# Second normalisation of a graph network: rows stored raw, factors kept, residuals normalised on load

## The chip, the core and the metric

The kernel runs on one core of a Trainium2 chip. The time is device time of one launch in microseconds. The core has a matmul engine (PE), a vector engine (DVE), a scalar engine (ACT), a general engine (POOL) that also builds the descriptors of indirect transfers, and SP, whose queue issues most plain transfers. Every engine works through its own instructions in order and meets the others through semaphores.

## The reference

There are N = 100,000 nodes with D = 128 features and E = 50,000 edges. Four residual blocks follow one another, each closed by a plain layer norm over the features:

```python
x = _layernorm(x + gcn2(x, edges))                 # block 0: two graph convolutions
x = _layernorm(x + gated(x, edges, edge_attr))     # block 1
x = _layernorm(x + attention(x, edges, edge_attr)) # block 2
x = _layernorm(x + gcn6(x, edges))                 # block 3: six convolutions, then @ Wf + bf

# gated: msg = sigmoid(z @ Wf.T + bf) * softplus(z @ Ws.T + bs); agg = sum of msg by dst
#        h = relu(LN(batchnorm(agg) + x) * gamma + beta);  returns h + x
# attention (3 heads): xp = x @ W; alpha = leaky_relu(a_src[row] + a_dst[col] + a_edge)
#        weights = softmax of alpha over the edges into a node (its own loop among them)
#        y = (sum of weights * xp[row] + bias) @ lin_W + lin_b;  returns LN(x + y) * g + b
```

Block 1 ends in two norms one after the other (its own, then the block's), and so does block 2. "First norm" and "second norm" below mean these two.

## The kernel before

Rows come in two kinds. The a rows (`rows_a`, 4 of 128 a block, 99 blocks `NBA`) are nodes with incoming edges, laid out with the sorted edges; the b rows (`rows_b`, 8 of 128 a block, 98 blocks `NB`) are all nodes, computed as if they had no edges. Both lie in one table, the b rows from row NA on. A block is 512 or 1024 rows.

The kernel is a chain of passes with a barrier after each. Every pass gives each engine a list of stages `(function, lag, blocks)` for `pipeline`: in turn t, stage f works on block t - lag, in the order of the list. So a stage's place is its lag (which turn) and its place in the list (where in the turn). Tiles have two, three or four buffers, and a semaphore wait with `b.after(k)` keeps k buffers apart. The passes and where they lie in the profiled span:

- first pass (0 to 666 us): sorts edges, makes weights (`weight_steps`, one product for each DVE turn), degree factors.
- graph passes 1 and 2 (to 2120.8): block 0.
- gated edge pass (to 2942.0): messages of block 1.
- gated node pass (`cn_`, to 4068.5): both norms of block 1 for a and b rows together, then transposes and the attention scores of each row. POOL has `batch_norm` and `gain`; DVE `stats_1`, `factors_1`, `shift`, `rectify`, `stats_2`, `factors_2`, `scores`; ACT `normalise_1`, `normalise_2` (both through `scale`, L1797, one activation for each 128 rows), the roots and `evacuate`; PE `turn` and `score`. `normalise_2` writes the tile o, which is stored as x2 and transposed.
- attention-gather pass (`ga_`, to 4856.6): b rows of block 2 (`AttentionNode` with `self_w`), while POOL gathers the scores of each edge's source (`att_e`, L2239).
- softmax pass (`sm_`, to 4941.2): DVE on [128, 3, 392] tiles; ends with `weight_own` and `weight_e`, the weights of own rows and edges.
- attention pass (`gb_`, to 6054.9): a rows of block 2. POOL gathers source rows and makes `own_w` (L2532, own rows times weights) and `x_beta` (L2165); ACT weighs the gathered rows (L2651); DVE sums them (`gb_run`, L2573), adds own rows (`gb_u`, L2595, in `add_own`), then `rows` adds bias and x again (`gb_a_r`, L2604, L2607), then norms. SP loads x2 twice: `load` for `own_w`, and `load_again` for `gb_a_r` and `x_beta`. `normalise_2` writes o, stored as x3 and transposed for the first weight of block 3.
- graph passes 3 to 8 (to 6590.9, 7121.0, 7640.1, 8160.6, 8683.3 and the end): a rows of block 3, one convolution a pass, with source rows gathered by POOL (L1370) into four tiles. The b rows' layers ride along as other `Node`s. The last layer of the b rows ("deep": convolution, last weight, residual x3, norm) is split over passes 5, 6 and 7, a block every 8/3 turns; that of the a rows is pass 8. `last_rows` (L1100) adds the residual `res_s`, loaded by `load_residual` (L1007).

In the attention pass SP's order is this (L2557):

```python
pipeline(sp, [(load, 0, NBA), (store_sums, 1, NBE), (load_again, 2, NBA), (n.store, 7, NBA),
              (n.store_next, 9, NBA)])
```

## Time and profile before

| what | us |
|---|---|
| median of 3 runs (9745.97 to 9760.18) | 9747.93 |
| profiled execution | 9742.82 |
| its span | 9741.1 |
| gated node pass, 2942.0 to 4068.5 | 1126.5 |
| attention-gather pass, to 4856.6 | 788.1 |
| softmax pass, to 4941.2 | 84.6 |
| attention pass, to 6054.9 | 1113.7 |
| graph passes 5, 6, 7 and 8 | 519.1, 520.5, 522.7, 1056.7 |

```profile
PE 6202.7 (64%) x32436; PEld 5087.5 (52%) x32436; DVE 7222.3 (74%) x22511; ACT 5612.8 (58%) x14065; POOL 7428.0 (76%) x6901
```

The line gives busy time, share of the span and instructions of each engine over the whole kernel. It is an average over fourteen passes with different work, so the passes are to be read one by one: their ends are the points at which all semaphores are cleared.

### The profile page before, as it was taken

The page shows a single profiled execution, that of the slowest core. Times are in us where ns is not written, and L with a number is a line of the kernel's source. Part 1 is how long each engine was busy: PE and PEld are TensorE (multiplying, and loading weights), DVE is VectorE, ACT ScalarE, POOL GpSimd, SP SyncE. Part 2 cuts the span into 40 slices and gives each one's busy share as a digit, 9 for nine tenths or more (in the row PEclk, how much of TensorE's full clock was granted, in tenths as well). Part 3 has the DMA queues.
Part 4 walks back from the last instruction along what each step waited for, and adds up shares of the span by engine and source line. Part 5 has one row for each costly group of instructions (what it writes and reads, how often), then busy time and mean ns, then how long its engine had stood idle before and what let it go on. Part 6 is the DMA issues. An engine that isn't in the chain of part 4 may idle for free. (4 is left out here: it accounts for less than half of the span.)

```text
span 9741.1 us, 131313 instructions
## 1 busy us (share of the span) xinstructions
PE 6202.7 (64%) x32436; PEld 5087.5 (52%) x32436; DVE 7222.3 (74%) x22511; ACT 5612.8 (58%) x14065; POOL 7428.0 (76%) x6901
## 2 busy tenths in 40 slices
PE   7017766668874666788746666884467675654444
PEld 3016656557764666688746665772244453432222
DVE  8349989978887777699878887655568776864444
ACT  0016667768888999899858876331135443432222
POOL 7757678878868888688657775777777777777777
PEclk9559988889995555688768887665568666765555
DMA  3999988863336777555435554663356443432222
GB/s 100 330 301 316 317 284 311 309 224 106 106 94 224 242 241 240 164 173 174 151 114 183 184 183 153 177 174 87 95 144 188 127 122 106 145 103 67 67 67 62
DMA packets 1024294, 1693.84 MB, mean 174 GB/s; under 512 B 301776, under 2 KB 544662, under 8 KB 1023475
## 3 DMA queue, kind: packets, MB, share of 16 engines
q1 hardware_dynamic: 797008, 1380.40, 41.9%
q0 software_dynamic: 166560, 199.56, 9.6%
q10 hardware_dynamic: 59970, 105.49, 3.1%
q8 instruction: 270, 4.42, 0.2%
q14 instruction: 486, 3.97, 0.1%
HBM read 988.10 MB, written 707.84 MB: 174 GB/s over the span
## 5 line engine op out<-in xcount | busy, mean ns | idle before, releaser
L1370 POOL DMA_INDIRECT g_got<-scaled,row_src x2352 | 2227.3, 947 | 787.1 <-issue 663.1
L922 DVE SCALAR_TENSOR_TENSOR g_sums<-g_got,first,g_sums 128x128 f32<-128x128 f32 (+3 forms) x3136 | 871.8, 278 | 1137.0 <-DMA g_got<-scaled,row_src 1126.8
L301 PE MATMUL g_a_p_z<-sb_L_gnn_W,g_a_u_t 128*128 128x128 f32 (+3 forms) x2574 | 585.4, 364 | 561.7 <-ACT g_a_u_t L1203 186.7
L926 DVE SCALAR_TENSOR_TENSOR g_sums<-g_sums,cont,g_got 128x128 f32<-128x128 f32 (+3 forms) x3128 | 879.7, 281 | 0.0
L1203 ACT COPY g_a_u_t<-g_a_p_t 128x512 f32<-128x512 f32 (+3 forms) x495 | 225.1, 455 | 1101.4 <-PE g_a_p_t L1155 643.6
L301 PE MATMUL g_bb_p_z<-sb_L_gnn_W,g_bb_u_t 128*128 128x128 f32 (+2 forms) x4302 | 759.4, 337 | 115.0 <-DVE g_bb_z L1097 56.9
L301 PEld LDWEIGHTS g_a_p_z<-sb_L_gnn_W,g_a_u_t 128*128 128x128 f32 (+1 forms) x2574 | 429.5, 238 | 729.4 <-ACT g_a_u_t L1203 404.2
L301 PEld LDWEIGHTS g_bb_p_z<-sb_L_gnn_W,g_bb_u_t 128*128 128x128 f32 x4302 | 668.2, 235 | 173.6 <-issue 145.3
L1203 ACT COPY g_bb_u_t<-g_bb_p_t 128x1024 f32<-128x1024 f32 (+2 forms) x294 | 233.9, 796 | 840.6 <-PE g_bb_p_t L292 837.0
L1527 POOL DMA_INDIRECT cg_got_src<-x,row_src x392 | 503.3, 1284 | 119.5 <-issue 119.5
L2512 POOL DMA_INDIRECT gb_got<-x,row_src x392 | 413.5, 1055 | 226.6 <-POOLq L179 122.6
L462 POOL DMA_INDIRECT f_got<-in_x,idx_dst x396 | 459.9, 1161 | 134.5 <-issue 120.4
L292 PE MATMUL g_bb_p_t<-ident,g_bb_own 128*128 128x128 f32 x2151 | 360.4, 308 | 297.7 <-DMA g_bb_own<-in_x 214.1
L1370 POOL DMA_INDIRECT g_got<-xs,idx_src x392 | 370.2, 944 | 231.2 <-issue 70.7
L2239 POOL DMA_INDIRECT att_e<-att,row_src x392 | 411.5, 1050 | 143.7 <-issue 105.2
L2635 PE MATMUL gb_p_m<-head_w,gb_u_t 128*128 128x128 f32 x2376 | 405.4, 347 | 127.2 <-DVE gb_a_r L2607 118.0
L1270 POOL DMA_INDIRECT out<-g_a_o,idx_out x396 | 390.5, 986 | 120.3 <-issue 120.0
L1370 POOL DMA_INDIRECT g_got<-wide,row_src x392 | 371.8, 948 | 137.2 <-issue 104.8
L292 PEld LDWEIGHTS g_bb_p_t<-ident,g_bb_own 128*128 128x128 f32 x2151 | 288.3, 164 | 345.7 <-DMA g_bb_own<-in_x 226.6
L1231 ACT ACTIVATE g_bb_o<-g_bb_z 128x1024 f32<-128x1024 f32 (+3 forms) x294 | 196.1, 667 | 470.5 <-DVE g_bb_z L1097 470.4
L2635 PEld LDWEIGHTS gb_p_m<-head_w,gb_u_t 128*128 128x128 f32 x2376 | 387.2, 258 | 139.0 <-issue 74.1
L1155 PE MATMUL g_a_p_t<-ident,g_a_own 128*64 128x128 f32 x396 | 104.9, 420 | 464.2 <-DVE g_a_own L1052 464.2
(501 smaller groups left out, 22496.3 us busy)
## 6 DMA issues: line engine op xcount, KB each, us to landing
raw<-gb_u SPq DMA_DIRECT2D x98, 768.0 KB, 3.9
xs<-f_o ACTq DMA_DIRECT2D x97, 516.0 KB
f_x<-in_x ACTq DMA_DIRECT2D x97, 512.0 KB
g_bb_own<-in_x SPq DMA_DIRECT2D x97, 512.0 KB
wide<-g_bb_o SPq DMA_DIRECT2D x97, 512.0 KB
g_bb_own<-wide SPq DMA_DIRECT2D x97, 512.0 KB
g_bb_res<-in_x SPq DMA_DIRECT2D x97, 512.0 KB
x<-g_bb_o SPq DMA_DIRECT2D x97, 512.0 KB
```

What stands on the lines that cost most here:

```text
L292: last = nc.tensor.transpose(dst_psum[0:n * k, q * P:q * P + p], tile[0:p, q * g * k:(q * g + n) * k], ident[0:p, 0:p])
L301: last = nc.tensor.matmul(dst_psum[0:p, q * g * width:(q * g + n) * width], turned_tile[0:n * k, q * P:q * P + p], weight[0:n * k, 0:n * w ...
L462: pool.indirect_dma_start(got[b.s4][:, c * D:(c + 1) * D], None, a["x"], bass.IndirectOffsetOnAxis(ap=idx_dst[:, b.n * CH + c:b.n * CH + c ...
L922: nc.vector.scalar_tensor_tensor(out=self.firsts, in0=new, scalar=first[:, col], in1=self.firsts, op0=ALU.mult, op1=ALU.add).then_inc(run_ ...
L926: nc.vector.scalar_tensor_tensor(out=self.part(b.s, c), in0=before, scalar=cont[:, col], in1=new, op0=ALU.mult, op1=ALU.add).then_inc(run_ ...
L1203: last = nc.scalar.copy(to, source)
L1270: nc.gpsimd.indirect_dma_start(self.to, bass.IndirectOffsetOnAxis(ap=idx_out[:, b.n * CH + c:b.n * CH + c + 1], axis=0), self.o_s[b.s4][:, ...
L1370: pool.indirect_dma_start(got[b.s4][:, c * row:(c + 1) * row], None, table, bass.IndirectOffsetOnAxis(ap=index[:, b.n * CH + c:b.n * CH + ...
L1527: pool.indirect_dma_start(got[b.s4][:, c * D:(c + 1) * D], None, x1, bass.IndirectOffsetOnAxis(ap=index[:, b.n * CH + c:b.n * CH + c + 1], ...
L2239: pool.indirect_dma_start(att_e[:, 4 * (b.n * CH + c):4 * (b.n * CH + c + 1)], None, att, bass.IndirectOffsetOnAxis(ap=row_src[:, b.n * CH ...
L2512: pool.indirect_dma_start(got[b.s4][:, c * D:(c + 1) * D], None, x2, bass.IndirectOffsetOnAxis(ap=row_src[:, b.n * CH + c:b.n * CH + c + 1 ...
L2635: last = nc.tensor.matmul(p_m[:, c * D:(c + 1) * D], u_t[h][:, c * P:(c + 1) * P], head_w[:, h * D:(h + 1) * D], start=(h == 0), stop=(h = ...
```

## The change

The second norm of blocks 1 and 2 is no longer applied to the rows before they are stored. x2 and x3 now hold the raw sums y. The second norm's factors (one root and one shift for each row) stay in SBUF for the rest of the kernel: `root2`, `shift2`, `root3`, `shift3`, found by `factor(t, r, b)`.

- Gated node pass: `normalise_2` and the tiles o are gone; y is stored (stage 6, was 7) and transposed (6, was 7). The scores are multiplied by `root2` in `scores` (8, was 9). A new ACT stage `put_roots` writes the row's root into the fourth column of the score table. `normalise_1` waits for the store of four blocks before.
- Weights that meet raw rows are centred over the input features with `centre_in` in the first pass, which takes the mean out; five matmuls and their evictions more.
- Softmax pass: `weight_e` is multiplied by the source row's root, `weight_own` by the own row's.
- Attention-gather pass: ACT's `settle` normalises the loaded rows in place (stage 1, last in ACT's turn); transposes and all that follows lie one stage later; four tiles for the load. `normalise_2` is gone.
- Attention pass: the first load is used raw. `load_again` has four tiles, lies at stage 1 (was 2) and stands ahead of `store_sums`; `settle` (stage 2, last in ACT's turn) normalises it; `rows` and `add_beta` wait for it. `normalise_2` is gone. `factors_2` has one more multiply, `by_root` = root times `inv`, with which `out_rows` scales.
- Graph passes 5 to 8: `settle` normalises the loaded residual x3 on ACT, at stage 4 for the b rows (its load at 2, was 3) and at stage 1 for the a rows; `last_rows` waits for it.

```diff
@@ first pass @@
+                        for t in (*[head_w[:, h * D:(h + 1) * D] for h in range(3)], score_w[:, :], w["L3_gnn_W1"][:, :]):
+                            emit(lambda o, t=t: nc.tensor.matmul(o, centre_in[:, :], t, start=True, stop=True), tuple(t.shape), t)
...
+                            done(nc.vector.tensor_scalar(centre_in[:, :], ident[:, :], -1.0 / D, None, ALU.add))
@@ Node (graph passes) @@
-                nc.vector.wait_ge(m.loaded_c[b.s], (b.pair + 1) * DMA)
+                nc.vector.wait_ge(m.settled, b.n + 1)
...
+            def settle(self, b):
+
+                p, j = self.r.pj(b)
+                m, res = self.m_, self.res_s[b.s]
+                nc.scalar.wait_ge(m.loaded_c[b.s], (b.pair + 1) * DMA)
+                roots, shifts = factor(root3, self.r, b), factor(shift3, self.r, b)
+                for q in range(j):
+                    last = nc.scalar.activation(res[0:p, q * D:(q + 1) * D], res[0:p, q * D:(q + 1) * D], ACT.Identity,
+                                                bias=shifts[:, q:q + 1], scale=roots[:, q:q + 1])
+                last.then_inc(m.settled, 1)
...
-                return self.on(lag, every, (self.load, 0), *([(self.load_residual, 3 if self.deep else 1)] if self.normal else []))
+                return self.on(lag, every, (self.load, 0), *([(self.load_residual, 2 if self.deep else 1)] if self.normal else []))
...
-                    return self.on(lag, every, (self.normalise, 8), (self.evacuate_b, 2), (self.root, 6), (self.evacuate, 1)), []
+                    return self.on(lag, every, (self.normalise, 8), (self.evacuate_b, 2), (self.root, 6), (self.evacuate, 1), (self.settle, 4)), []
...
-                            stages = ahead + in_a((na.normalise, 3), (na.evacuate_b, 1), (na.evacuate, 0), (na.root, 2)) + behind
+                            stages = ahead + in_a((na.normalise, 3), (na.evacuate_b, 1), (na.evacuate, 0), (na.root, 2), (na.settle, 1)) + behind
@@ gated node pass @@
-                    sp.wait_ge(m.normed_b, b.n + 1)
-                    sp.dma_start(self.r.rows(x2, b, self.base()), split(self.o_s[b.s], p, j)).then_inc(m.stored[b.s], DMA)
+                    sp.wait_ge(m.summed_b, b.n + 1)
+                    sp.dma_start(self.r.rows(x2, b, self.base()), split(self.y_s[b.n % 4], p, j)).then_inc(own_stored[b.s4], DMA)
...
                     if b.after(4):
-                        act.wait_ge(m.normed_b, b.n - 3)
+                        act.wait_ge(own_stored[b.s4], b.turn * 2 * DMA)
+                        act.wait_ge(m.turned, b.n - 3)
...
-                def normalise_2(self, b):
+                def put_roots(self, b):
...
-                        act.wait_ge(m.stored[b.s], b.pair * DMA)
-                        act.wait_ge(m.turned, b.n - 1)
-                    self.n2.scale(self.o_s[b.s], self.y_s[b.n % 4], b, self.first, p, j).then_inc(m.normed_b, 1)
+                        act.wait_ge(m.stored_b[b.s], b.pair * DMA)
+                    nc.scalar.copy(split(self.att_s[b.s], p, j, 4)[:, :, 3], factor(root2, self.r, b)).then_inc(m.settled, 1)
...
-                                       (na.normalise_2, 6, NBA), (nb.normalise_2, 6, NB), (na.evacuate, 7, NBA),
-                                       (nb.evacuate, 7, NB)])
+                                       (na.evacuate, 6, NBA), (nb.evacuate, 6, NB), (na.put_roots, 7, NBA), (nb.put_roots, 7, NB)])
...
-                        pipeline(pe, [(na.turn, 7, NBA), (nb.turn, 7, NB), (na.score, 8, NBA), (nb.score, 8, NB)])
+                        pipeline(pe, [(na.score, 7, NBA), (nb.score, 7, NB), (na.turn, 6, NBA), (nb.turn, 6, NB)])
@@ AttentionNode @@
+                if self.a:
+                    nc.vector.tensor_tensor(self.by_root[b.s4][:, :], roots, at_window(inv, b), ALU.mult)
...
+                act.wait_ge(again_loaded[b.s4], (b.turn + 1) * DMA)
+                x = self.x_r[b.s4]
+                roots, shifts = factor(root2, self.r, b), factor(shift2, self.r, b)
+                for q in range(j):
+                    last = nc.scalar.activation(x[0:p, q * D:(q + 1) * D], x[0:p, q * D:(q + 1) * D], ACT.Identity,
+                                                bias=shifts[:, q:q + 1], scale=roots[:, q:q + 1])
+                last.then_inc(m.settled, 1)
@@ attention-gather pass @@
-                        pipeline(act, [(evacuate, 2, NB), (n.root_2, 6, NB), (n.normalise_1, 4, NB), (n.root_1, 3, NB),
-                                       (n.evacuate_out, 7, NB), (n.normalise_2, 6, NB)])
+                        pipeline(act, [(evacuate, 3, NB), (n.root_2, 7, NB), (n.normalise_1, 5, NB), (n.root_1, 4, NB),
+                                       (n.evacuate_out, 8, NB), (n.settle, 1, NB)])
@@ softmax pass @@
+                        by_source = att_e[:, :].rearrange("p (t f) -> p f t", f=4)[:, 3:4, :].to_broadcast([P, H, T])
+                        nc.vector.tensor_tensor(weight_e[:, :, :], weight_e[:, :, :], by_source, ALU.mult)
+                        by_own = root2[:, :].rearrange("p (n g) -> p n g", g=BOTH)[:, :, 0:CH]
+                        for h in range(H):
+                            own_h = split(weight_own[:, h, :], P, NBA, CH)
+                            last = nc.vector.tensor_tensor(own_h, own_h, by_own, ALU.mult)
+                        done(last)
@@ attention pass @@
-                            if b.after(2):
-                                sp.wait_ge(m.rows_ready, b.n - 1)
-                                sp.wait_ge(m.gained, b.n - 1)
-                            sp.dma_start(split(n.x_r[b.s], P, CH), r.rows(x2, b)).then_inc(m.loaded_b[b.s], DMA)
+                            if b.after(UNROLL):
+                                sp.wait_ge(m.rows_ready, b.n - 3)
+                                sp.wait_ge(m.gained, b.n - 3)
+                            sp.dma_start(split(n.x_r[b.s4], P, CH), r.rows(x2, b)).then_inc(again_loaded[b.s4], DMA)
...
-                        pipeline(sp, [(load, 0, NBA), (store_sums, 1, NBE), (load_again, 2, NBA), (n.store, 7, NBA),
+                        pipeline(sp, [(load, 0, NBA), (load_again, 1, NBA), (store_sums, 1, NBE), (n.store, 6, NBA),
                                       (n.store_next, 9, NBA)])
...
-                                       (n.normalise_1, 4, NBA), (n.normalise_2, 6, NBA)])
+                                       (n.normalise_1, 4, NBA), (n.settle, 2, NBA)])
```

## Rows read from the trace of the kernel before

**Rows 1.** Busy time by pass: stretch in us: its length, then busy us of each engine (instructions), clock, DMA.

```profile
2942.00:4068.50 1126.50, 711.15 (x3534) 685.31 (x3534) 865.75 (x2572) 1084.25 (x2751) 950.04 (x592) 0.54 0.70 232
4068.50:4856.60 788.10, 663.71 (x4692) 637.15 (x4692) 721.38 (x1468) 748.54 (x1956) 643.30 (x490) 0.83 0.53 165
...
4941.20:6054.90 1113.70, 750.87 (x4754) 694.73 (x4754) 921.34 (x1681) 855.74 (x2563) 837.03 (x789) 0.82 0.53 175
...
8160.60:8683.30 522.70, 327.54 (x1225) 215.94 (x1225) 411.96 (x1646) 197.66 (x460) 396.58 (x441) 0.72 0.45 132
8683.30:9740.00 1056.70, 503.45 (x1388) 276.21 (x1388) 482.09 (x1581) 306.85 (x693) 820.14 (x887) 0.51 0.24 66
```

**Rows 2.** Timeline of ACT in the gated node pass: start us, length us, operation.

```profile
3400.93 0.48 ACT L1783 ACTIVATE cn_n_sd<-cn_n_stats,cn_eps 128x12 f32<-128x12 f32 x1
...
3405.96 1.80 ACT L1797 ACTIVATE cn_a_o<-cn_a_y,cn_n_nmr,cn_n_rstd 128x128 f32<-128x128 f32 x4
3407.49 3.33 ACT L1797 ACTIVATE cn_b_o<-cn_b_y,cn_n_nmr,cn_n_rstd 128x128 f32<-128x128 f32 x8
```

**Rows 3.** Timeline of POOL in the gated node pass, with idle time before and its releaser.

```profile
3403.61 1.27 POOL L1890 TENSOR_TENSOR cn_a_y<-cn_a_y,cn_half 128x512 f32<-128x512 f32 x1
3406.10 2.35 POOL L1890 TENSOR_TENSOR cn_b_y<-cn_b_y,cn_half 128x1024 f32<-128x1024 f32 x1 [1.21 <-ACT cn_b_y L1797]
...
3414.64 1.27 POOL L1890 TENSOR_TENSOR cn_a_y<-cn_a_y,cn_half 128x512 f32<-128x512 f32 x1
```

**Rows 4.** Timeline of ACT in the attention-gather pass.

```profile
4404.73 0.99 ACT L2298 COPY ga_x_t<-ga_p_x 128x1024 f32<-128x1024 f32 x1
...
4412.35 1.00 ACT L2298 COPY ga_x_t<-ga_p_x 128x1024 f32<-128x1024 f32 x1
```

**Rows 5.** Waits in the attention pass, 5150 to 5700 us: total us, times, longest.

```profile
POOL gb_own_w L2532 <- DMA gb_a_x<-x: 59.2, 50, 2.5
...
DVE gb_a_r L2607 <- DMA gb_a_x_r<-x: 45.7, 51, 2.9
```

**Rows 6.** Timeline of DVE in the attention pass.

```profile
5408.15 1.76 DVE L2595 TENSOR_TENSOR gb_u<-gb_run,gb_own_w 128x1536 f32<-128x1536 f32 x1 [0.24 <-DVE gb_run L2573]
...
5410.35 0.60 DVE L348 SCALAR_TENSOR_TENSOR gb_a_n_nmr<-gb_a_n_stats,gb_a_n_rstd 128x4 f32<-128x4 f32 x1
...
5414.52 0.69 DVE L2607 TENSOR_TENSOR gb_a_r<-gb_a_r,gb_a_x_r 128x512 f32<-128x512 f32 x1 [0.80 <-DMA gb_a_x_r<-x]
...
5418.77 1.76 DVE L2595 TENSOR_TENSOR gb_u<-gb_run,gb_own_w 128x1536 f32<-128x1536 f32 x1 [0.24 <-DVE gb_run L2573]
```

**Rows 7.** Waits in the seventh graph pass, 8220 to 8620 us.

```profile
POOL g_got L1370 <- issue: 87.6, 304, 0.3
...
DVE g_sums L922 <- DMA g_got<-scaled,row_src: 52.0, 35, 3.0
```

**Rows 8.** The page's DMA issues: count, KB each, median us from issue to landing.

```profile
raw<-gb_u SPq DMA_DIRECT2D x98, 768.0 KB, 3.9
```

**Rows 9.** Groups by line, attention-gather pass, 4250 to 4650 us: busy us, mean ns, idle before.

```profile
L2165 POOL TENSOR_TENSOR ga_b_x_beta<-ga_b_x,row_L_gnn_ln_b 128x1024 f32<-128x1024 f32 x53 | 125.7, 2372 | 0.9
...
L2154 DVE COPY ga_b_g<-ga_b_p_g 128x512 f32<-128x512 f32 x53 | 34.2, 644 | 0.0
...
L348 DVE SCALAR_TENSOR_TENSOR ga_b_n_nmr<-ga_b_n_stats,ga_b_n_rstd 128x8 f32<-128x8 f32 x52 | 8.7, 167 | 1.8
```

**Rows 10.** Timeline of POOL in the attention pass.

```profile
5409.65 1.27 POOL L2165 TENSOR_TENSOR gb_a_x_beta<-gb_a_x_r,row_L_gnn_ln_b 128x512 f32<-128x512 f32 x1
...
5417.23 3.04 POOL L2532 TENSOR_TENSOR gb_own_w<-gb_a_x,weight_own 128x512 f32<-128x512 f32 x3 [1.08 <-DMA gb_a_x<-x]
```

**Rows 11.** Timeline at the end of the softmax pass.

```profile
4939.35 1.38 DVE L2469 TENSOR_TENSOR weight_e<-sm_power,sm_spread_v 128x1176 f32<-128x1176 f32 x1
```

**Rows 12.** Timeline of DVE late in the first pass.

```profile
517.46 0.21 DVE L774 TENSOR_SCALAR gate_w<-gate_w 17x128 f32<-17x128 f32 x1
...
662.28 0.95 DVE L785 TENSOR_TENSOR f_o<-f_x,f_inv 112x768 f32<-112x768 f32 x1
```

More of the change, by code:

```diff
@@ L1530, in gather @@
                                     ).then_inc(ready[b.s4], DMA)
[L1532 removed]
+                        pool.wait_ge(m.loaded[0], DMA)
                         pool.indirect_dma_start(
@@ L1750, in build, with factor @@
         gated_edge_pass()
+        BOTH = CH + J
+        root2, shift2, root3, shift3 = (keep(n, [P, NBA * BOTH]) for n in ("root2", "shift2", "root3", "shift3"))
+        def factor(t, r, b):
+            at = (r.start + b.n) * BOTH + (0 if r.name == "a" else CH)
+            p, j = r.pj(b)
+            return t[0:p, at:at + j]
         def gated_node_pass():
@@ L1816, in __init__ @@
                     self.y_s = [sb(f"{n}_y{s}", [P, G * D]) for s in range(4)]
-                    self.o_s = [sb(f"{n}_o{s}", [P, G * D]) for s in two]
                     self.att_s = [sb(f"{n}_att{s}", [P, G * 4]) for s in two]
@@ L1863, in stores_done @@
                     for s in range(2):
-                        nc.sync.wait_ge(self.m.stored[s], blocks_in(self.r.blocks, s) * DMA)
                         nc.sync.wait_ge(self.m.stored_b[s], blocks_in(self.r.blocks, s) * DMA)
@@ L1996, in _ @@
                         nb.stores_done()
+                        for s in range(UNROLL):
+                            sp.wait_ge(own_stored[s], (blocks_in(NBA, s, UNROLL) + blocks_in(NB, s, UNROLL)) * DMA)
                     @block.gpsimd
@@ L2065, in __init__ @@
                 two = range(2)
-                self.x_s = [sb(f"{n}_x{s}", [P, G * D]) for s in (two if self.a else range(3))]
-                self.x_r = [sb(f"{n}_x_r{s}", [P, G * D]) for s in two] if self.a else self.x_s
+                if self.a:
+                    self.x_s = [sb(f"{n}_x{s}", [P, G * D]) for s in two]
+                self.x_r = [sb(f"{n}_x_r{s}", [P, G * D]) for s in range(UNROLL)]
                 self.x_beta = [sb(f"{n}_x_beta{s}", [P, G * D]) for s in range(4)]
                 self.r_s = [sb(f"{n}_r{s}", [P, G * D]) for s in two]
-                self.y_s = [sb(f"{n}_y{s}", [P, G * D]) for s in range(3)]
-                self.o_s = [sb(f"{n}_o{s}", [P, G * D]) for s in two]
+                self.y_s = [sb(f"{n}_y{s}", [P, G * D]) for s in range(4)]
+                self.by_root = [sb(f"{n}_by_root{s}", [P, G]) for s in range(UNROLL)]
                 self.g_s = [sb(f"{n}_g{s}", [P, G * H1]) for s in two]
@@ L2086, in store @@
                 m, sp = self.m, nc.sync
-                sp.wait_ge(m.normed_b, b.n + 1)
-                sp.dma_start(self.r.rows(x3, b, self.base()), split(self.o_s[b.s], p, j)).then_inc(m.stored[b.s], DMA)
+                sp.wait_ge(m.summed_b, b.n + 1)
+                sp.dma_start(self.r.rows(x3, b, self.base()), split(self.y_s[b.s4], p, j)).then_inc(own_stored[b.s4], DMA)
             def store_next(self, b):
@@ L2098, in stores_done @@
                 for s in range(2):
-                    nc.sync.wait_ge(self.m.stored[s], blocks_in(self.r.blocks, s) * DMA)
                     nc.sync.wait_ge(self.m.stored_b[s], blocks_in(self.r.blocks, s) * DMA)
+                for s in range(UNROLL):
+                    nc.sync.wait_ge(own_stored[s], blocks_in(self.r.blocks, s, UNROLL) * DMA)
             def stats_1(self, b):
@@ L2158, in add_beta @@
                 m, pool = self.m, nc.gpsimd
[L2159 to L2162 removed]
+                pool.wait_ge(m.settled, b.n + 1)
                 if b.after(4):
                     pool.wait_ge(m.summed_b, b.n - 3)
[L2165 removed]
+                nc.gpsimd.tensor_tensor(split(self.x_beta[b.s4], p, j), split(self.x_r[b.s4], p, j),
                                         row_of(brow["L2_gnn_ln_b"], p, j), ALU.add).then_inc(m.gained, 1)
@@ L2251, in load @@
                             p, j = r.pj(b)
-                            if b.after(3):
-                                sp.wait_ge(m.gained, b.n - 2)
-                                sp.wait_ge(m.turned, b.n - 2)
-                            sp.dma_start(split(n.x_s[b.n % 3], p, j), r.rows(x2, b, NA)).then_inc(m.loaded[b.n % 3], DMA)
-                        pipeline(sp, [(load, 0, NB), (n.store, 6, NB), (n.store_next, 8, NB)])
+                            if b.after(UNROLL):
+                                sp.wait_ge(m.gained, b.n - 3)
+                                sp.wait_ge(m.turned, b.n - 3)
+                            sp.dma_start(split(n.x_r[b.s4], p, j), r.rows(x2, b, NA)).then_inc(again_loaded[b.s4], DMA)
+                        pipeline(sp, [(load, 0, NB), (n.store, 7, NB), (n.store_next, 9, NB)])
                         n.stores_done()
@@ L2519, in gather_firsts @@
                             if at_end(b):
-                                for s in range(UNROLL):
-                                    pool.wait_ge(raw_stored[s], blocks_in(NBE, s, UNROLL) * DMA)
+                                for s in two:
+                                    pool.wait_ge(sums_stored[s], blocks_in(NBE, s) * DMA)
                                 pool.indirect_dma_start(firsts[:, :], None, raw,
```

130 lines of the change are left out of this document (68 added, 62 removed).

## The prediction

> **What bounds the kernel now.** I split the span at the ends of the passes and read busy time by pass [rows 1], since the kernel has no single bound. Each pass that the change touches then gets its own look: the timeline of the fullest engine over two turns, and the list of waits.
>
> The gated node pass has 99 turns. ACT is busy for 1084 of 1126.5 us. In the timeline it runs without a gap: four second-norm scalings of the a rows take 1.53 us from start to start, so 0.383 us each, and the eight of the b rows follow [rows 2]. A turn lasts 11.03 us on POOL, from 3403.61 to 3414.64, and POOL waits once in it, 1.21 us, for ACT's first norm of the b rows [rows 3]. So POOL needs 9.82 us a turn. DVE has 865.75/99 = 8.7 us of work, PE 7.2 [rows 1].
>
> The attention-gather pass is as full: ACT repeats after 7.62 us [rows 4] and is busy for 749 of 788 us; DVE has 721/98 = 7.36 us a turn [rows 1].
>
> In the attention pass no engine is full (DVE 921, ACT 856, POOL 837 of 1114 us, [rows 1]), so a loop sets the turn. The waits show it: DVE waits 45.7 us over 51 turns for the second load of x (0.90 a turn), POOL 59.2 us over 50 turns for the first load (1.18) [rows 5]. The timeline closes the loop. gb_u ends at 5408.15 + 1.76 = 5409.91. SP stands at store_sums, which waits for it, and issues the second load only behind it. The tile lands 4.6 us later, at 5414.52, after DVE has stood 0.80 us. DVE then needs 6.0 us to the next end of gb_u, at 5420.53. The turn is 10.62 us [rows 6].
>
> The later graph passes are bound by POOL's gathers. In the seventh POOL stops only for issue (87.6 us in 400), never for another engine, and DVE waits for gathered rows (52.0 us) [rows 7].
>
> **Gated node pass.** Twelve scalings leave ACT: 1.53 + 8 x 0.383 = 4.6 us a turn. Two small put_roots copies come, at most 0.48 us each like the small root beside them [rows 2]: +1.0. ACT falls to 11.0 - 4.6 + 1.0 = 7.4 us. POOL is late next, at 9.82 us, and is not changed; DVE's score copies become multiplies of the same few elements. Gain: 1.21 us x 95 turns (99, less the first four, in which POOL has no gain stage) = 115 us, and 4.6 us more in the drain, where the last block no longer has a second norm between sums and transposes. Together 120. The lower end of the gain is 60: half of it, if the transfers, busy for 0.70 of the pass, stretch when it shrinks to 1007 us (0.78). The store leaves one stage earlier and waits for the sums of the turn before, where load_again already waits for them, so SP isn't held longer. The first norm now waits for a store two turns ahead of it, against a landing of about 4 us [rows 8]. PE scores ahead of its transposes; 7.2 us of PE work in 9.8 leaves room for that order.
>
> **Attention-gather pass.** ACT swaps eight scalings for eight of the same shape (settle), so it stays at 7.62 us. DVE's copy of 512 columns from PSUM, 644 ns [rows 9], becomes a multiply; DVE's operation of that width takes 0.69 us [rows 6]. So +0.05: 7.41 us, still hidden behind ACT by 0.2. If the cover were gone it would cost 98 x 0.05 = 5 us. The transposes now wait for settle instead of the load, but lie one stage later; the settle at the start (3.1 us) replaces the second norm in the drain. Cost 0, between -5 and +10.
>
> **Attention pass.** load_again moves ahead of store_sums, a stage earlier, with four tiles. Behind the wait of store_sums stand now the two stores and the next first load; the second load no longer. That takes DVE's 0.90 us away. settle takes the place of the second norm on ACT and no longer waits for DVE's factors of the same turn; its result is wanted a turn later. What is late next? DVE without that wait is at 10.62 - 0.90 = 9.72, POOL without its own at 10.62 - 1.18 = 9.44 us. POOL's wait for x stands behind gb_u as before: own_w starts at 5417.23 for gb_u's end at 5409.91, 7.32 us later, and own_w with 3.04 us and x_beta with 1.27 end 4.3 us after that start [rows 10].
>
> One DVE operation matters here: nmr takes 0.60 us, from 5410.35 to 5410.95 [rows 6], and POOL's x_beta ends at 5410.92 [rows 10]. In the attention-gather pass the same operation takes 167 ns [rows 9]. I read this as DVE held by POOL. The new by_root multiply stands just ahead of nmr and is held with it. From x_beta's end to gb_u's end lie 9.61 - 0.80 = 8.81 us. If the turn is P, x_beta ends (lag + 4.3 - P) after gb_u, so P = lag + 4.3 - P + 8.81. With the lag of now, 7.32, P is 10.2 us. With 256 KB less ahead of x in the queue, a third of a 768 KB store's 3.9 us or 1.3 at most [rows 8], the lag is 6.0 and P 9.56. POOL's floor is 9.44. I take 9.9, near the middle. Gain: (10.62 - 9.9) x 97 = 70 us, between 41 (10.2) and 114 (9.44).
>
> The Trainium skill (SBUF — State Buffer, "Who interferes with whom") says that a DVE instruction with two SBUF inputs contends with a GpSimd instruction that reads SBUF, by an exclusive lock. By that rule nmr and by_root are held as above, and the sum stands; without such a lock P would be 9.72 or less and the sum 18 us better.
>
> **Softmax pass.** One more multiply of 1176 columns, 1.38 us [rows 11], and three of 396, by width 0.46 us each: +2.8, all on the chain that ends the pass. Between 2 and 4.
>
> **Graph passes five to eight.** ACT gets eight scalings (3.06 us) for each of 98 deep blocks and four (1.53 us) for each of 99 blocks in the last pass. ACT in the seventh pass rises from 198 to 298 of 523 us, in the eighth from 307 to 458 of 1057 [rows 1]. POOL's gathers hide it, with four tiles of lead. The residual's load is asked a stage earlier than before in passes five to seven, and with a deep block only every 8/3 turns its tile is free then. Cost 0, upper bound 20 (a fifth of 100 us in which the operation could hold PE's or DVE's next step).
>
> **First pass.** Five more weight products and a constant come one to each DVE turn. These steps end at 517.46 now and the pass's last scaling starts at 662.28 [rows 12]; six turns of some 4.2 us end them near 543. Cost 0; uncovered it would be 25 us.
>
> **Sum.** -120 - 70 + 3 = -187. The profiled execution took 9742.82 us (span 9741.1), the median of three is 9747.93, 5 us more. 9747.9 - 187 = **9561 us**.
>
> **Rivals.**
> (A) The attention pass gains nothing: POOL's wait for x, or ACT, takes the place of DVE's wait and the turn stays 10.62. For it: two loads are waited for and only one is moved. Against it: gb_u(n) needs own_w(n) only two turns after the release of x(n), 21 us, of which lag and own_w take 10.4. 9561 + 70 = 9631.
> (B) The gated node pass is held by its transfers or by DVE's chain, and gains half: 9561 + 60 = 9621. Against it: DMA share 0.70 and DVE 8.7 us.
> (C) The attention-gather pass, where three engines lie within 4%, loses its rhythm: POOL's x_beta, 2.37 us [rows 9], falls on DVE's two additions from SBUF, and DVE stands for part of it. At 1 us a turn, 9561 + 98 = 9659.
> (D) Slower: settle in graph passes five to seven. It stands ahead of the a rows' evacuation on ACT. If all its 3.06 us reach DVE's combine and through it POOL's gathers, the 98 deep blocks cost 300 us: 9861. It decides from 187/98 = 1.9 us a block. Against it: in the seventh pass DVE still waits for gathers 52 us in 400, and POOL leads by up to four blocks.
>
> By that page of the Trainium skill, SBUF — State Buffer, "Who interferes with whom", (C) is what its lock could cost; no row here shows DVE held in that pass.
>
> **How the numbers follow.** Forecast 0.60 (its own range 9515 to 9600), A 0.17, B 0.11, C 0.07, D 0.05 (most of it slower, a little of it in between). A difference under 0.2% (19 us) can't be told from none. Faster 0.94, same 0.02, slower 0.04. The forecast's own range comes from P at 9.44 and 10.2. For 8 in 10 I reach from 9520 to 9650: this takes in A and B and leaves out C, D and the far ends.
>
> **What would show it.** Right: the gated node pass takes some 1007 us, its ACT about 0.7 busy, POOL without a gap at 9.8 us a turn. The attention pass takes about 1045 us with no DVE wait for x_r, nmr and by_root still stretched, POOL still waiting for x. The attention-gather pass stays at 788, the softmax pass at 87, passes five to eight within 2 us of before. Wrong: a DVE wait on settle (r or the last rows), ACT waiting for the second load, POOL in a graph pass waiting for g_sums, or x_beta stretching DVE in the attention-gather pass.

## The result and the profile after

| | median us | lowest to highest, runs |
|---|---|---|
| before | 9752.51 | 9745.97 to 9760.18, 4 |
| after | 9597.19 | 9595.60 to 9613.28, 4 |

The ratio is 0.9844, with a 95% interval of 0.9832 to 0.9855: 155 us or 1.6% faster. The forecast was 9561 us, 36 us too low. The profiled execution after took 9598.75 us, its span 9596.9.

First the busy time by pass of the kernel after, as in [rows 1] (stretch in us: its length, then busy us of PE, PEld, DVE, ACT, POOL with instructions, clock, DMA): the gated node pass, attention-gather, the attention pass, and the graph passes 5, 6 and 7.

```profile
2949.40:3949.00 999.60, 745.27 (x3534) 708.58 (x3534) 863.66 (x2573) 680.40 (x1770) 945.78 (x592) 0.54 0.82 261
3949.00:4744.70 795.70, 638.34 (x4692) 617.62 (x4692) 723.48 (x1468) 748.08 (x1956) 645.42 (x490) 0.85 0.53 163
...
4833.00:5871.90 1038.90, 719.87 (x4754) 661.93 (x4754) 951.51 (x1780) 852.49 (x2563) 869.15 (x789) 0.85 0.57 188
...
6934.10:7473.50 539.40, 373.20 (x1486) 255.02 (x1486) 417.57 (x1738) 352.59 (x804) 396.68 (x441) 0.76 0.58 168
7473.50:8014.50 541.00, 387.83 (x1223) 251.47 (x1223) 367.43 (x1647) 298.65 (x726) 396.59 (x441) 0.53 0.39 105
8014.50:8536.80 522.30, 328.56 (x1225) 214.85 (x1225) 410.71 (x1646) 295.99 (x722) 396.61 (x441) 0.72 0.46 132
```

The span fell by 144.2 us (9741.1 to 9596.9), and the medians by 155, since single executions of one kernel spread over 14 to 18 us. Against the lengths of before this is where the 144 us went (0.8 us lie behind the last stretch):

| pass | predicted | measured |
|---|---|---|
| gated node | -120 | -126.9 |
| attention-gather | 0 | +7.6 |
| softmax | +2.8 | +3.7 |
| attention | -70 | -74.8 |
| graph 5 and 6 | 0 | +20.3 and +20.5 |
| graph 7 and 8 | 0 | -0.4 and +1.5 |
| the other six | 0 | +3.5 |

Two big terms came as forecast. The surprise is in graph passes 5 and 6, with 41 us.

**Gated node pass.** The timeline of POOL after, as in [rows 3]:

```profile
3500.74 1.27 POOL L1918 TENSOR_TENSOR cn_a_y<-cn_a_y,cn_half 128x512 f32<-128x512 f32 x1
...
3510.51 1.27 POOL L1918 TENSOR_TENSOR cn_a_y<-cn_a_y,cn_half 128x512 f32<-128x512 f32 x1
```

The 1.21 us wait for ACT is gone, and a turn lasts 9.77 us, POOL's own work. ACT is busy for 680 us of 1000; before, it was for 1084 of 1126.

**Attention pass.** The timeline of DVE after, as in [rows 6], from one `gb_u` to the next:

```profile
5300.53 1.76 DVE L2643 TENSOR_TENSOR gb_u<-gb_run,gb_own_w 128x1536 f32<-128x1536 f32 x1 [0.24 <-DVE gb_run L2621]
...
5302.74 0.97 DVE L2176 TENSOR_TENSOR gb_a_by_root<-root,inv 128x4 f32<-128x4 f32 x1
...
5303.71 0.68 DVE L2153 TENSOR_TENSOR gb_a_y<-gb_a_y,row_L_gnn_ln_g 128x512 f32<-128x512 f32 x1
...
5306.60 0.69 DVE L2655 TENSOR_TENSOR gb_a_r<-gb_a_r,gb_a_x_r 128x512 f32<-128x512 f32 x1
...
5310.84 1.76 DVE L2643 TENSOR_TENSOR gb_u<-gb_run,gb_own_w 128x1536 f32<-128x1536 f32 x1 [0.24 <-DVE gb_run L2621]
...
5313.04 0.62 DVE L2176 TENSOR_TENSOR gb_a_by_root<-root,inv 128x4 f32<-128x4 f32 x1
...
5320.80 1.76 DVE L2643 TENSOR_TENSOR gb_u<-gb_run,gb_own_w 128x1536 f32<-128x1536 f32 x1 [0.24 <-DVE gb_run L2621]
```

No wait for the second load is left. The turns are 10.31 and 9.96 us. The multiply `by_root`, of four elements a row, is stretched to 0.97 and 0.62 us. And POOL in the same stretch, as in [rows 10]:

```profile
5302.41 1.28 POOL L2199 TENSOR_TENSOR gb_a_x_beta<-gb_a_x_r,row_L_gnn_ln_b 128x512 f32<-128x512 f32 x1
5303.83 1.41 POOL L2560 DMA_INDIRECT gb_got<-x,row_src  x1
5305.55 0.95 POOL L2560 DMA_INDIRECT gb_got<-x,row_src  x1 [0.30 <-issue]
5306.80 1.30 POOL L2560 DMA_INDIRECT gb_got<-x,row_src  x1 [0.30 <-issue]
5308.41 0.94 POOL L2560 DMA_INDIRECT gb_got<-x,row_src  x1 [0.31 <-issue]
5309.37 3.03 POOL L2580 TENSOR_TENSOR gb_own_w<-gb_a_x,weight_own 128x512 f32<-128x512 f32 x3
```

`x_beta` ends at 5303.69, just where `by_root` ends (5303.71): DVE stood until POOL was through. Then look at the four gathers. Two take 0.95 us, two 1.41 and 1.30, and those two began while DVE was in an operation with both inputs in SBUF (a multiply, 5303.71 to 5304.39, and an addition, 5306.60 to 5307.29). POOL still waits for x, but in 24 turns only, 19.6 us in all, after 122.0 us in 91 turns before. Its next turn, from this `own_w` to the one at 5319.34, is 9.97 us without a wait: 3.03 + 1.27 of tensor work, 4.6 of gathers and some 1.1 between them.

**Graph pass 6.** The timeline around one deep block:

```profile
7818.31 1.11 ACT L1222 ACTIVATE g_bc_h_t<-g_bc_p_t,col_L_gnn_b 128x1024 f32<-128x1024 f32 x1 [6.91 <-PE g_bc_p_t L1183]
7819.32 3.17 ACT L1232 ACTIVATE g_bc_res<-g_bc_res,shift,root 128x128 f32<-128x128 f32 x8
7822.40 0.25 ACT L1209 COPY g_a_u_t<-g_a_p_t 64x128 f32<-64x128 f32 x1
7822.58 1.22 DVE L1115 TENSOR_TENSOR g_bc_y<-g_bc_p_z,g_bc_res 128x1024 f32<-128x1024 f32 x1 [6.49 <-ACT g_bc_res L1232]
...
7829.22 0.95 POOL L1387 DMA_INDIRECT g_got<-scaled,row_src  x1 [2.97 <-DVE g_a_own L1066]
```

ACT stood 6.91 us for PE's transposed product (`evacuate_b`, L1222). `settle` lies behind that in ACT's list, though its tile has long been loaded. So DVE's `last_rows` waits 6.49 us, the a rows' evacuation comes after settle (7822.40), and the delay reaches POOL: the gather waits 2.97 us for a free tile. Over the pass these are two rows of the waits (total us, times, longest):

```profile
DVE g_bc_y L1115 <- ACT g_bc_res L1232: 65.9, 11, 6.6
...
POOL g_got L1387 <- DVE g_a_own L1066: 21.0, 10, 3.1
```

In pass 5 the way to POOL is another. DVE waits only 27.3 us for settle there, at most 2.5 at a time. But the evacuation of the other `Node` of b rows (`g_bb_u_t`) stands behind settle too, and PE's product from it (`g_bb_p_z`) waits 34.8 us for ACT, after 6.2 us before.

### The profile page after: what moved, and what is told of

The parts are those of the page before. It is cut to its first block and busy times, and to the rows that moved or that the text cites. A ratio compares the mean times of both kernels' runs of the same rounds, so it can differ in the third digit from the quotient of the medians.

```text
span 9596.9 us, 131552 instructions
## 1 busy us (share of the span) xinstructions
PE 6222.6 (65%) x32446; PEld 5085.1 (53%) x32446; DVE 7255.3 (76%) x22620; ACT 5641.1 (59%) x14262; POOL 7461.4 (78%) x6901
## 5 line engine op out<-in xcount | busy, mean ns | idle before, releaser
L2560 POOL DMA_INDIRECT gb_got<-x,row_src x392 | 445.9, 1137 | 237.1 <-POOLq L179 132.5
L1544 POOL DMA_INDIRECT cg_got_src<-x,row_src x392 | 471.9, 1204 | 119.4 <-issue 119.4
L2278 POOL DMA_INDIRECT att_e<-att,row_src x392 | 389.2, 993 | 133.5 <-issue 97.2
L2683 PE MATMUL gb_p_m<-head_w,gb_u_t 128*128 128x128 f32 x2376 | 375.4, 330 | 97.3 <-DVE gb_a_r L2655 88.9
L2683 PEld LDWEIGHTS gb_p_m<-head_w,gb_u_t 128*128 128x128 f32 x2376 | 358.6, 242 | 108.8 <-ACT gb_u_t L2708 88.7
```

The lines of the kernel that those rows point to most:

```text
L1544: pool.indirect_dma_start(got[b.s4][:, c * D:(c + 1) * D], None, x1, bass.IndirectOffsetOnAxis(ap=index[:, b.n * CH + c:b.n * CH + c + 1], ...
L2278: pool.indirect_dma_start(att_e[:, 4 * (b.n * CH + c):4 * (b.n * CH + c + 1)], None, att, bass.IndirectOffsetOnAxis(ap=row_src[:, b.n * CH ...
L2560: pool.indirect_dma_start(got[b.s4][:, c * D:(c + 1) * D], None, x2, bass.IndirectOffsetOnAxis(ap=row_src[:, b.n * CH + c:b.n * CH + c + 1 ...
L2683: last = nc.tensor.matmul(p_m[:, c * D:(c + 1) * D], u_t[h][:, c * P:(c + 1) * P], head_w[:, h * D:(h + 1) * D], start=(h == 0), stop=(h = ...
```

## The experiments

All are edits of the kernel after. Runs 2, 3 and 6 to 8 are single executions, beside a before of 9751.57 us (2 and 3) or 9761.39 (6 to 8); the runs with an interval had four executions against seven of before.

**1. Settle first on ACT.**

```diff
-  return self.on(lag, every, (self.normalise, 8), (self.evacuate_b, 2), (self.root, 6), (self.evacuate, 1), (self.settle, 4)), []
+  return self.on(lag, every, (self.settle, 4), (self.normalise, 8), (self.evacuate_b, 2), (self.root, 6), (self.evacuate, 1)), []
```

> Against the kernel before. Theory 1 (order): in graph passes five and six settle stands in ACT's list behind the evacuation of the multiplied block, which in every third deep block falls in the same turn and waits for PE; ACT idles up to 6.9 us with the residual landed and DVE's last rows wait 6.5 us. With settle first in the list passes five and six go from 539.4 and 541.0 us back to about 520, passes seven and eight stay, and the whole is near 9557 us. Theory 2 (load): it is the 3.1 us of added work for a deep block wherever it stands; then passes five and six stay at 540 and the whole at 9597.

It took 9566.07 us (before 9751.57), ratio 0.9811, interval 0.9795 to 0.9827. The first expectation, of the order, holds for the two passes; the whole is 9 us above it. The passes 5 and 6 by busy time:

```profile
6935.10:7455.20 520.10, 362.20 (x1486) 245.24 (x1486) 416.63 (x1738) 354.02 (x804) 397.66 (x441) 0.78 0.59 174
7455.20:7978.20 523.00, 353.48 (x1223) 237.37 (x1223) 367.64 (x1647) 298.79 (x726) 397.68 (x441) 0.60 0.40 108
```

ACT has the same 299 us of work in pass 6 and the pass is 18 us shorter, so it is the place in the list that makes this work cost time. In pass 5 PE waits 5.8 us for that evacuation and no longer 34.8. Against the kernel before, 1.0 and 2.5 us are left. The timeline of ACT shows it: settle runs in the time in which ACT would have waited for PE.

```profile
7775.44 3.18 ACT L1232 ACTIVATE g_bc_res<-g_bc_res,shift,root 128x128 f32<-128x128 f32 x8
7782.54 1.11 ACT L1222 ACTIVATE g_bc_h_t<-g_bc_p_t,col_L_gnn_b 128x1024 f32<-128x1024 f32 x1 [3.92 <-PE g_bc_p_t L1183]
```

The granted clock of pass 6 is 0.60 here, 0.59 before and 0.53 after, all between the levels of 1.2 and 2.4 GHz (0.5 and 1). It came back with the order; how much of the 18 us is the stall itself and how much matmuls at the lower clock, the runs don't separate.

**2. One scaling in place of eight (four), at the place of the kernel after.** This kernel leaves out the other scalings, so its results aren't the reference's; it is there for its time alone.

```diff
-  for q in range(j):
+  for q in range(1):
```

> Leaves out seven of eight (b rows) and three of four (a rows) scalings of the residual in graph passes five to eight; the rest of the order stays as after the change. Theory 1 (order): a settle of 0.5 us still waits behind the evacuation, up to 6.9 us less of its own 3.1, so passes five and six recover only in part: between 522 and 532. Theory 2 (load): both are back at 520. Passes seven and eight stay in both.

One execution took 9552.91 us, with the passes 5 and 6 at

```profile
6929.60:7448.80 519.20, 366.40 (x1486) 245.17 (x1486) 417.42 (x1738) 269.63 (x580) 396.63 (x441) 0.78 0.60 174
7448.80:7970.20 521.40, 367.63 (x1223) 243.40 (x1223) 368.39 (x1647) 209.83 (x495) 396.66 (x441) 0.57 0.39 109
```

ACT's wait for PE in `evacuate_b` is still there (125.6 us in pass 6), with settle behind it, but hardly anything of the loss: 0.1 and 0.9 us against the kernel before. The number is that of the second theory, load, as that of run 1 was that of the first. So neither the order nor the 3.1 us of work is enough by itself. In pass 6 DVE's wait for settle is

```profile
DVE g_bc_y L1115 <- ACT g_bc_res L1232: 22.5, 10, 3.9
```

and POOL's for `g_a_own` is 1.4 us, after 65.9 and 21.0 in the kernel after, and none and 1.4 in run 1. The wait behind the evacuation and the work added to it together reach POOL, and each alone is covered.

**3. Twelve scalings back on ACT in the gated node pass**, into spare tiles for which nobody waits.

```diff
+                for q in range(j):
+                    last = nc.scalar.activation(self.spare[b.s][0:p, q * D:(q + 1) * D], bn_shift[0:p, :], ACT.Identity,
+                                                bias=eps[0:p, :], scale=eps[0:p, :])
...
+                                       (na.scale_spare, 6, NBA), (nb.scale_spare, 6, NB),
```

> Puts twelve scalings of 128 columns back on ACT in each turn of the gated node pass, written to spare tiles that nobody reads, at the place of the old second norm, so ACT has the old work and nobody waits for it. Theory (ACT set the turn): the turn goes from 9.77 us to 11.3 us (6.7 + 4.6, or 11.0 with the shorter small operations), the pass from 1000 to between 1110 and 1140 us. Rival (the waits around the second norm set it, not its work): the pass stays under 1030 us.

One execution took 9743.81 us. The pass, and POOL's wait for ACT in it:

```profile
2946.60:4084.60 1138.00, 769.70 (x3534) 730.32 (x3534) 872.23 (x2573) 1103.41 (x2948) 950.09 (x592) 0.55 0.74 229
```

```profile
POOL cn_b_y L1920 <- ACT cn_b_y L1827: 124.9, 89, 1.8
```

ACT is full again (1103 of 1138) and POOL's wait for it is back at 1.4 us a turn. The store's later wait, PE's new order and the missing tiles weigh nothing beside this: the gain of the pass is ACT's work. (The pass is 12 us longer than before; ACT has the two `put_roots` copies a turn besides, and the run doesn't separate what they cost.)

**4. The factors later in DVE's turn** of the attention pass.

```diff
-  (add_own, 1, NBA), (n.out_rows, 8, NBA), (n.factors_2, 6, NBA),
-  (n.gain, 5, NBA), (n.add_x, 5, NBA), (n.stats_2, 5, NBA), (n.factors_1, 3, NBA)
+  (add_own, 1, NBA), (n.out_rows, 8, NBA),
+  (n.gain, 5, NBA), (n.add_x, 5, NBA), (n.factors_2, 6, NBA), (n.stats_2, 5, NBA), (n.factors_1, 3, NBA)
```

> In the attention pass only, the second norm's factors stand behind the two additions on DVE's list instead of ahead of them, so that by_root starts after POOL's x_beta has ended. Theory 1 (DVE, held by POOL, sets the turn of 9.96 us): by_root falls from 0.67 to 0.17 us and the turn by 0.4 us, the pass from 1039 to about 1000. Theory 2 (POOL sets it: it has no wait left, and its gathers are stretched by DVE's additions from SBUF): by_root falls, but the turn stays at 9.9 to 10.0 and the pass within 8 us.

9593.40 us, ratio 0.9837 (0.9821 to 0.9854); the pass 1035.5 us. The timeline of DVE, then that of POOL:

```profile
5285.65 1.72 DVE L2153 TENSOR_TENSOR gb_a_y<-gb_a_y,row_L_gnn_ln_g 128x512 f32<-128x512 f32 x1
...
5296.06 0.93 DVE L2153 TENSOR_TENSOR gb_a_y<-gb_a_y,row_L_gnn_ln_g 128x512 f32<-128x512 f32 x1
...
5297.84 0.16 DVE L2176 TENSOR_TENSOR gb_a_by_root<-root,inv 128x4 f32<-128x4 f32 x1
...
5299.44 0.70 DVE L2655 TENSOR_TENSOR gb_a_r<-gb_a_r,gb_a_x_r 128x512 f32<-128x512 f32 x1
```

```profile
5285.53 1.28 POOL L2199 TENSOR_TENSOR gb_a_x_beta<-gb_a_x_r,row_L_gnn_ln_b 128x512 f32<-128x512 f32 x1
...
5295.17 1.27 POOL L2199 TENSOR_TENSOR gb_a_x_beta<-gb_a_x_r,row_L_gnn_ln_b 128x512 f32<-128x512 f32 x1
...
5299.41 0.95 POOL L2560 DMA_INDIRECT gb_got<-x,row_src  x1 [0.30 <-issue]
```

The second theory holds: the pass moved by 3 us. `by_root` is 0.16 us, and `gain`, now the first operation with two SBUF inputs, is held in its stead (1.72 and 0.93 in these two turns, 1.24 in the mean of the pass, 0.68 without a hold). So the hold isn't bound to one instruction: it takes whichever such instruction meets `x_beta`. Nor did it get smaller: DVE is busy for 951.9 us in the pass, and for 951.5 in the kernel after. The gathers are shorter (mean 1025 ns, after 1137), because the addition at 5299.44 now starts 0.03 us behind the gather and neither is held. But POOL's wait for x is back, 59.4 us over the pass, after 19.6. One was given for the other.

**5. `x_beta` ahead of `own_w` on POOL.**

```diff
-  pipeline(pool, [(gather, 0, NBE), (weigh_own, 1, NBA), (gather_firsts, 1, NBA), (n.add_beta, 4, NBA)])
+  pipeline(pool, [(gather, 0, NBE), (n.add_beta, 4, NBA), (weigh_own, 1, NBA), (gather_firsts, 1, NBA)])
```

> In the attention pass only, POOL's add_beta stands ahead of weigh_own instead of behind it. Theory (the turn of 9.96 us is set by a loop through the hold: own_w starts 6.5 to 7 us after gb_u, and the first DVE operation with two inputs in SBUF behind gb_u stands until own_w and x_beta have ended): x_beta then runs before x lands, own_w ends 1.3 us earlier against gb_u, the hold of by_root falls below 0.3 us, the turn to POOL's floor of 9.5, the pass from 1039 to about 1000. Rival (DVE's or ACT's own work sets it): the turn stays within 0.1 us of 9.96 and the pass within 10 us of 1039.

9598.74 us, ratio 0.9836 (0.9819 to 0.9852); the pass 1030.6 us. POOL's wait for x is gone (7.2 us in all), yet the turn is 9.95 us and not the 9.5 expected. In its numbers that is the rival. The timeline of POOL:

```profile
4997.83 1.40 POOL L2560 DMA_INDIRECT gb_got<-x,row_src  x1 [0.16 <-issue]
...
5000.78 1.30 POOL L2560 DMA_INDIRECT gb_got<-x,row_src  x1 [0.30 <-issue]
```

So 9.95 us is POOL's own sum of work with the gathers as DVE stretches them, where the prediction had POOL's floor at 9.44. But DVE waits for no other engine in this turn either, with `by_root` held to 0.62 us. Each engine is held by the other, and the run doesn't say which of the two sets the turn.

**6 and 7. Where the second load is issued**: behind `store_sums` at stage 1, and behind it at stage 2 (the old place) with the four tiles and settle kept.

```diff
-  pipeline(sp, [(load, 0, NBA), (load_again, 1, NBA), (store_sums, 1, NBE), (n.store, 6, NBA),
+  pipeline(sp, [(load, 0, NBA), (store_sums, 1, NBE), (load_again, 1, NBA), (n.store, 6, NBA),      # 6
+  pipeline(sp, [(load, 0, NBA), (store_sums, 1, NBE), (load_again, 2, NBA), (n.store, 6, NBA),      # 7
```

> In the attention pass only, load_again stays at stage 1 with four tiles but stands behind store_sums as before the change. Theory (the stage brings the gain): the rows land 4.6 us after the end of gb_u, settle and gb_a_r come a turn later, so nothing waits and the pass stays at 1039 within 10. Rival (the place ahead of store_sums brings it): DVE waits for settle about 1 us a turn and the pass is 1110 or more.

> As e6, but load_again also back at stage 2, as before the change, with four tiles and settle kept. Theory: the loop of before returns with settle in it; 4.6 us to landing, 1.6 us of settle and 6.0 us of DVE make a turn of at least 12.2 us, the pass 1240 us or more. Rival A of the prediction (the second load didn't set the turn): under 1060 us. If ACT and DVE catch up otherwise, about 1114.

The first took 9616.86 us, the pass 1063.9; the second 9866.72 us, the pass 1295.5. The waits of the second over the pass:

```profile
ACT gb_a_x_r L2230 <- DMA gb_a_x_r<-x: 395.5, 97, 7.8
POOL gb_own_w L2580 <- DMA gb_a_x<-x: 310.9, 94, 8.1
DVE gb_a_r L2655 <- ACT gb_a_x_r L2230: 308.3, 97, 5.9
```

At the old stage and place, with settle, the pass is 182 us longer than before the change: ACT waits for the load, DVE for ACT, `gb_u` for DVE, and SP issues the next load behind `gb_u`. The loop of the prediction is there, and the turn came as the first theory of this run has it (at least 12.2 us a turn, 1240 us). With the stage moved alone, run 6, 50 of the 75 us gained are kept (1113.7 - 1063.9), and the place ahead of `store_sums` brings the other 25. Run 6 met neither expectation, since it lies between them.

**8. The kernel before once more**, for the spread of passes that the change hardly touches.

> The kernel before, profiled once more. The first pass and graph pass one read 11 us longer in the profile after the change than in the one before. Theory 1: that is spread between executions, and this one lies 3 us or more above the first profile in one of the two passes. Theory 2: the six further steps of the first pass and later code cost it; then this one repeats 666.4 and 592.6 us within 1 us each.

The first pass took 669.5 us, after 666.4 in the first profile, and the first graph pass 593.7 after 592.6, so they differ by 3 and 1 us between two executions of one kernel. In the kernel after they are 6 and 5 us longer than in the first profile. Half of the 6 is in that spread, and the kernels with the change ran the first pass in 667.1 to 672.5 us, so no cost of the six further steps is shown. What lengthened the first graph pass to 597.5 us stays open.

**9 to 11. Together.** Settle first with the beta addition ahead; settle first with the later factors; all three.

> Both single changes together: the settling of the node pass first on ScalarE's list, and GpSimd's addition of beta ahead of its weighing. If the two passes are independent the savings add: passes 5 and 6 of the graph at 520 and 523 us as with the settling first alone (from 539 and 541), the attention's node pass at 1031 us as with the addition ahead alone (from 1039), attention-gather 790, so about 9556 us. Rival: the earlier settling moves the attention pass too, so that the addition brings nothing on top: 1036 to 1040 us in that pass and 9564 to 9568 us in all.

> The settling of the node pass first on ScalarE's list, and VectorE's factors later in its turn. If the savings add: the passes 5 and 6 at 520 and 523 us, the attention's node pass at 1036 us, about 9562 us in all. If GpSimd's own sum of work bounds that pass, as the run with the factors later alone suggested, the pass can't fall below 1030 us here either, and the time is within 5 us of 9566 us.

> All three single changes: the settling of the node pass first on ScalarE's list, GpSimd's addition of beta ahead of its weighing, and VectorE's factors later in its turn. If GpSimd's sum of work bounds the attention's node pass and only stretched gathers keep it above its bare sum, the later factors move a two-input addition off the gathers' starts: the pass falls to between 1000 and 1025 us (a turn of 9.6 to 9.85 us) and the whole to between 9530 and 9550 us. Rival: some two-input operation of VectorE meets GpSimd's long operation or the start of a gather in any order, and the pass stays at 1030 to 1036 us, the whole at 9550 to 9560 us.

| run | median us | ratio, interval | attention pass |
|---|---|---|---|
| 9 | 9558.14 | 0.9801, 0.9785 to 0.9818 | 1032.0 |
| 10 | 9552.95 | 0.9795, 0.9778 to 0.9811 | 1035.8 |
| 11 | 9511.41 | 0.9759, 0.9743 to 0.9775 | 990.1 |

Run 9 came as expected in its median; the attention-gather pass of its profiled execution took 843.1 us and not 790, as told at the end. In run 10 the three passes came as expected (519.6, 521.6 and 1035.8 us) and the whole 9 us below. Run 11 went past its range, and shows what the two edits of the attention pass do to each other. POOL's gathers in the groups by line of that pass (busy us, mean ns, idle before), and two `gb_u` in the timeline of DVE:

```profile
L2560 POOL DMA_INDIRECT gb_got<-x,row_src x392 | 400.1, 1021 | 235.4 <-POOLq L179 130.6 <-issue 101.3
```

```profile
5124.71 1.76 DVE L2643 TENSOR_TENSOR gb_u<-gb_run,gb_own_w 128x1536 f32<-128x1536 f32 x1 [0.24 <-DVE gb_run L2621]
...
5134.17 1.76 DVE L2643 TENSOR_TENSOR gb_u<-gb_run,gb_own_w 128x1536 f32<-128x1536 f32 x1 [0.24 <-DVE gb_run L2621]
```

Run 4 had the short gathers and a wait for x; run 5 had no wait for x and long gathers. They gained 3 and 8 us in the pass, and neither is clear of the spread in the whole. With both, the turn is 9.46 us, where neither DVE nor POOL waits for another engine, and 49 us are gained (1038.9 - 990.1). Little of either hold is left in these turns: `gain` takes 0.75 us, and only the first gather of four is stretched, to 1.25. Run 11 is the best version: 86 us under the kernel after.

## Why the prediction was right, and by how much it was off

**Gated node pass: right.** Forecast 1007 us, ACT at 0.7, POOL without a gap at 9.8; measured 999.6, 0.68 and 9.77. Run 3 shows the cause. The term was 7 us short, 5 of them in the drain: from POOL's last `gain` of the a rows to the end of the pass before took 38.1 us (4030.4 to 4068.5) and now 28.3 (3920.7 to 3949.0), 9.8 less where 4.6 were forecast. A `put_roots` copy takes 0.2 us and not 0.48, which is why ACT is at 6.9 us a turn and not at 7.4; POOL sets the turn, so that gave nothing.

**Attention pass: right in size, with a mis-sized part.** From the first to the last of 98 `gb_u` before took 1041.2 us (4958.3 to 5999.5) and now 972.6 (4850.3 to 5822.9), 10.73 and 10.03 us a turn; the forecast was 10.62 to 9.9. The loop through `store_sums` is shown by runs 6 and 7, the held DVE by run 4. But the bound at the other end was wrong. "POOL without its own at 10.62 - 1.18 = 9.44 us" left out that POOL's gathers grow when the turn moves them against DVE's additions: their mean went from 1055 to 1137 ns, and in the turns shown four of them take 4.60 us and not 4.16. POOL's own work at that phase is 9.95 us a turn (run 5). The forecast also had POOL still waiting for x in each turn, by which its equation gives P; it waits in 24 turns only. P = 9.9, taken near the middle between two bounds, was near the measured turn for another reason than that given, so the size of this term was partly luck. A turn near the 9.44 was reached only in run 11, with another order.

The Trainium skill (SBUF — State Buffer, "Who interferes with whom") says of the port pair that DVE shares with GpSimd that the order of issue decides who is blocked. The trace agrees: a gather that starts 0.2 us behind the addition takes 1.30, one that starts 0.03 us ahead of it 0.95 (runs 5 and 4). But the same section of the Trainium skill infers that a `tensor_tensor` doesn't hold the making of descriptors. These 1.30 us say otherwise, and the measurement decides.

**Softmax pass: right.** +3.7 for 2.8. The multiply of `weight_e` by every fourth element of the score tile takes 2.24 us and not the 1.38 of one with dense inputs:

```profile
4829.07 2.24 DVE L2510 TENSOR_TENSOR weight_e<-weight_e,att_e 128x1176 f32<-128x1176 f32 x1
```

**Attention-gather pass: the turn right, the ends not.** ACT still repeats after 7.62 us, and the 98 copies of `x_t` begin within 734.2 us, from the first to the last (3962.0 to 4696.2), before 736.1 (4075.3 to 4811.4). But the step "the settle at the start (3.1 us) replaces the second norm in the drain" fails: at the start ACT settles two blocks before its first copy. The timeline of ACT after:

```profile
3955.81 6.26 ACT L2230 ACTIVATE ga_b_x_r<-ga_b_x_r,shift,root 128x128 f32<-128x128 f32 x16 [10.37 <-DMA ga_b_x_r<-x]
3961.98 0.99 ACT L2337 COPY ga_x_t<-ga_p_x 128x1024 f32<-128x1024 f32 x1
```

The first copy comes 13.0 us into the pass and not 6.8, so 6.2 us are lost. The drain is 3.3 us longer too (48.5 for 45.2), not shorter. Other kernels with the same pass ran it in 790.2 to 796.4 us, before in 788.1 and 786.9 (run 8); the cost is between 2 and 10 us.

**Graph passes 5 and 6: the step that failed.** "POOL's gathers hide it, with four tiles of lead ... Cost 0, upper bound 20": the cost is 41 us. The prediction compared ACT's busy time (298 of 523 us) with the pass and took the rest as cover. It did not ask what stands ahead of settle in ACT's list: a wait of up to 7 us for PE. Its evidence against a cost, DVE's wait for gathered rows and POOL without a wait for others, was read from pass 7 [rows 7], the one of the three in which POOL isn't reached. Rival D had the mechanism, and the place nearly; its price was that of every block, and POOL was reached only in some ten places of a pass, by about 2 us each (in pass 6 it waits 21.0 us in 10 for the a rows' `g_a_own`, in pass 5 16.1 us in 10 for `g_sums`). Its lead of four tiles would cover the rest. The price of these few was not worked out. Passes 7 and 8 are as forecast. In pass 7 the same stages wait the same way (DVE 40 us for settle, at most 5.3 at a time) and POOL is hardly reached (1.9 us); why it isn't there stays open. Its granted clock is 0.72, that of pass 6 is 0.53, which may shorten the wait for PE, but no run separates that.

**Rivals.** A (attention pass gains nothing) and B (gated half) did not occur. C is not in the kernel after, whose `x_beta` in the attention-gather pass is held by DVE (2645 ns, before 2372 [rows 9]) and not DVE by it. It did occur in one execution of run 9, described below.

The sum: the profile of before less the forecast gain gives a span of 9741.1 - 187 = 9554, and measured were 9597, 43 us more. That is +41, +7.6 and +0.9, then -7 and -5, and +5 in the passes that were put at nothing.

## What to carry to other kernels

When work is added to an engine with idle time, the question is not only how much is idle but what the stage is queued behind: here work whose input had long been there cost 3 to 4 us over two passes at the head of the turn, and 41 us behind a stage that waits. And when a wait is removed, the next bound should be read with its operations at the phase that they will then have; two edits that were worth 3 and 8 us alone were worth 49 together. In a pass that has to fill its stages first, count how many blocks the new stage does before the old first one.

## What the runs showed of the hardware that was not expected

**A gather's issue is held by DVE.** An indirect transfer whose issue takes POOL 0.95 us takes 1.25 to 1.41 when it starts during a DVE multiply or addition with both inputs in SBUF (kernel after, runs 4, 5 and 11). In the turns shown it is longer by a little less than what is left of that operation when it starts: in the kernel after 0.46 us for 0.56, and 0.36 for 0.49. It isn't that the first gather behind POOL's tensor work is slow by itself: in the turns of run 7 in which that gather starts outside such an operation it takes 0.98 us.

**The same instructions in two rhythms.** The profiled execution of run 9 took 9598.23 us, the other three 9554.48 to 9559.90. The excess is in the attention-gather pass, 843.1 us, in which run 9 has the instructions of the kernel after. The timeline of that execution, DVE and then POOL:

```profile
4305.65 0.90 DVE L2177 SCALAR_TENSOR_TENSOR shift<-ga_b_n_stats,root 128x8 f32<-128x8 f32 x1
```

```profile
4304.15 2.37 POOL L2199 TENSOR_TENSOR ga_b_x_beta<-ga_b_x_r,row_L_gnn_ln_b 128x1024 f32<-128x1024 f32 x1
4306.67 1.84 POOL L2278 DMA_INDIRECT att_e<-att,row_src  x1 [0.16 <-issue]
```

Here `x_beta` began first (4304.15): DVE's small `shift`, 167 ns in the kernel after, is held to 0.90 us until `x_beta` ends at 4306.52, DVE's multiply and addition behind it come later, and the gather that starts during the multiply is held to 1.84. This is rival C, though the operation held is the small one ahead of the two that it named; the pass is 47 us longer than in the kernel after. There DVE's addition begins first, and `x_beta` takes 2.65 us in its stead, for which nobody waits. What sets the order at the start of the pass was not found.
